# Layer 1's keys, values and masks of a two-layer attention kernel, made ahead of the layer instead of inside its steps

## The chip, the cores and the metric

The kernel runs on one core of one Trainium2 chip. The metric is the device time of one execution in microseconds (us). The core has a tensor engine (PE, with its weight loads listed as PEld), a vector engine (DVE), a scalar engine (ACT), GpSimd (POOL) and a sync engine (SP), which here issues nearly all DMAs. Each engine runs its own instruction list in order and waits on semaphores. Matmuls write PSUM, which has eight banks of 512 float columns a partition; everything else lives in SBUF.

## The reference, cut to what matters

Batches B = 32, sequence S = 128, width D = 128. Four stages change the residual x:

```
x = x + attn0(norm(x), ctx)            # 16 heads of 8, rotary, no mask
x = x + ffn0(norm(x))                  # 128 -> 512 -> 128, ternary weights
x = x + attn1(norm(x), ctx, mask)      # 16 query heads of 8, 4 key/value heads of 8
x = x + experts(norm(x))               # 8 experts, one chosen per token

attn1:  q = query @ Wq.T + bq ;  k = ctx @ Wk.T + bk ;  v = ctx @ Wv.T + bv   # k, v are 32 wide
        sim = where(causal & (adj != 0), q k^T / sqrt(8), -max) ;  softmax ; @ v ; layer norm ; @ Wo.T + bo
```

Keys, values and masks of attn1 depend on `ctx` and `adj` alone, which are inputs. They don't depend on x.

## The kernel before, in words

**The steps.** Each attention layer is a list of steps `step(t, j)`, one for a batch, with j = t mod 6. `attention(L)` (L529 on PE, L980 on ACT, L1257 on POOL, L1460 on DVE, L369 on SP) builds the step of one engine. In step t the engines work on different batches: PE makes the scores of batch t+2 (`scores`, L633), the transposed scores of t (`scoresT`, L658), the product with the values of t-1 (`pv`, L689), and the output product of t-2 (`out_project`, L745). Even steps also project the values (`project_v`, L597) and keys (`project_k`, L578) of a pair of batches, odd steps transpose the normalised x of a pair (`xn_transposes`, L538) and project its queries (`project_q`, L548). In layer 1 the odd step also makes the gate's base logits (`base_logits`, L566).

**The halves.** The scores of a batch have two halves of eight heads. Both use the one tile `score`, so `scores` of the next half waits until DVE has taken the row maxima of the last one (`maxima`, L1532, tile `negmax`). PE's order in a step is: scores half 0, scoresT half 0, pv, transposes of maxima (L729) and output (L736), then values or `xn` transposes, scores half 1, scoresT half 1, output product, regrouping (L713), then projections (L790 to L814). "First half" below is the time from scores half 0 to scores half 1 of a batch, "second half" the time from there to the next batch's half 0.

**Query and key pieces.** Queries and keys are float32, and each is cut into three bf16 pieces: ACT makes the whole (`whole`, L989, in layer 1) and the high piece (`high`, L1000), POOL the middle, the rest and the low piece (`cut`, L1272: lines L1281, L1282, L1284). SP then stacks them with six DMAs a pair of batches into `stack` (`stack_first`, `stack_last`, L404 and L415), each of which carries a query piece and a key piece. A blank row and the maxima's row (`max_rows`, L437) come in DMAs of their own. Both layers do this for every pair.

**Layer 1's masks.** For each pair SP loads `adj` (L385), DVE makes a bf16 mask (`make_mask`, L1514, line L1528; the triangle is read from PSUM, L728, from the fourth pair on), and SP copies its two halves of partitions crosswise into `swapped` (L427). PE adds both to the scores with matmuls (L619, L629). Layer 1's values come from a product of 32 columns for each batch (L608) and are put beside their bias into `Vc` by DVE (`values`, L1502).

**Between the layers.** `ffn(early)` runs 16 pairs (L817 on PE, L1143 on ACT, L1377 on POOL, L1761 on DVE). PE's pair: transposes (L825), up (L835), down (L845). From pair 8 on, each pair also runs one step of layer 1, from t = -8 on (`run_early`, L286). PE and ACT run pairs 2 to 7 in a loop (`pair_loop`, L319), and PE runs steps 6 to 23 of both layers in a loop of three rounds (`body_loop`, L291). After layer 0, SP issues four loads of expert weights (L475), a 896 KB write of zero rows (L478), and then waits for layer 1.

**In layer 1** POOL also has the bias of x (`add_bias`, L1308), reciprocal roots, and one or more indirect DMAs a step that scatter rows to the experts (`scatter`, L1334). DVE also ranks tokens, in units of two to six batches.

## Time and profile before

| | us |
|---|---|
| median of three runs (535.7 to 539.16) | 536.88 |
| the profiled execution | 535.18 |
| its span | 533.0 |
| PE busy in the span | 459.7 (86%) |
| DVE busy | 380.5 (71%) |
| POOL busy | 359.5 (67%) |
| ACT busy | 350.0 (66%) |

The span runs from the first to the last instruction of the profiled execution, and some 2 us lie around it. From the starts of the row maxima (line L1536), layer 0's attention takes the span up to about 165 us, the ffn up to 249 us (layer 1's first scores are at 240 us), layer 1's attention up to about 412 us. The experts' products begin at about 446 us. A row of the timeline gives start, duration, engine, line and operation; "x8" means that eight instructions were merged into one row. A figure in brackets is the idle time before it and what ended it.

### The profile page before, as it was taken

The numbers are of one execution on the slowest core, as the hardware profiler recorded it, in microseconds if no ns is written. First come the engines' busy times: TensorE is split into PE (matmuls) and PEld (weight loads), VectorE is DVE, ScalarE is ACT, GpSimd is POOL, SyncE is SP. The second block draws the span as 40 slices with busy tenths as digits, with TensorE's granted clock in tenths as the row PEclk, the third lists the DMA queues.
The fourth block names the chain that finished last, engine by engine and source line by source line (L and its number), as shares of the span: only waits on it lengthen the run. The fifth ranks groups of instructions, "written<-read, shape, count | busy, mean of one in ns | idle before, by whom it ended". The sixth has DMA issues, their size and how long they took to land.

```text
span 533.0 us, 19424 instructions
## 1 busy us (share of the span) xinstructions
PE 459.7 (86%) x6192; PEld 357.6 (67%) x6192; DVE 380.5 (71%) x1125; ACT 350.0 (66%) x872; POOL 359.5 (67%) x739
## 2 busy tenths in 40 slices
PE   3678999999988799998999999999978615999992
PEld 2456777777766699885566666666655405999991
DVE  6788888888986566535578888898898562555551
ACT  4366788888865556563677788788767713666661
POOL 5788887888842366577667776999986770555552
PEclk9799999999999999999799999999999955999997
DMA  7565445454432930034344444555442233444430
GB/s 182 146 160 147 109 121 124 115 138 114 124 77 59 337 85 0 1 91 104 94 114 119 127 122 113 149 146 146 126 126 70 74 121 86 106 108 108 106 99 23
DMA packets 103996, 60.18 MB, mean 113 GB/s; under 512 B 21234, under 2 KB 100098, under 8 KB 103922
## 3 DMA queue, kind: packets, MB, share of 16 engines
q1 hardware_dynamic: 100562, 51.92, 38.8%
q0 software_dynamic: 2784, 6.82, 3.7%
q8 instruction: 36, 0.59, 0.5%
q10 hardware_dynamic: 576, 0.53, 0.3%
q14 instruction: 38, 0.31, 0.2%
HBM read 20.03 MB, written 8.81 MB: 54 GB/s over the span
## 4 chain that ended last, share of the span: by engine, by line
PE 63%; POOL 11%; issue 8%; DVE 8%; DMA 5%; ACT 2%; SPq 1%; POOLq 0%; DVEq 0%; ACTq 0%
PE bank L702 8%; PE bank L923 6%; PE bank L845 5%; PE score L653 5%; PE scoreT L835 5%; PE scoreT L913 5%; PE bank L561 3%; POOL expert_rows L1341 3%; DVE negmax L1536 3%; PE bank L592 3%; PE bank L756 3%; DMA stack<-negpT 2%; PE scoreT L680 2%; PE score L913 2%; PE score L619 2%
## 5 line engine op out<-in xcount | busy, mean ns | idle before, releaser
L1536 DVE TENSOR_REDUCE negmax<-score 128x8 f32<-128x1024 f32 x128 | 156.2, 1220 | 36.1 <-PE score L653 34.1
L1028 ACT ACTIVATE P<-scoreT 128x1024 f32<-128x1024 f32 x128 | 131.7, 1029 | 51.4 <-PE scoreT L671 30.1
L702 PE MATMUL bank<-P,Vc 128*32 128x128 f32 x2048 | 69.2, 276 | 1.9 <-issue 1.8
L1420 POOL DMA_INDIRECT out<-by x39 | 37.5, 962 | 48.8 <-DVE by L1882 48.1
L702 PEld LDWEIGHTS bank<-P,Vc 128*32 128x32 f32 x2048 | 52.1, 109 | 15.4 <-issue 9.8
L653 PE MATMUL score<-stack 64*128 64x128 bf16 x1024 | 51.9, 222 | 6.9 <-DVE negmax L1536 4.5
L653 PEld LDWEIGHTS score<-stack 64*128 64x128 bf16 x1024 | 29.6, 95 | 37.8 <-issue 23.4
L1284 POOL TENSOR_TENSOR pieces<-rest,pieces 128x256 bf16<-128x256 f32 x63 | 42.8, 679 | 4.9
L1281 POOL TENSOR_TENSOR pieces<-full,pieces 128x256 bf16<-128x256 f32 x63 | 42.3, 672 | 4.7 <-ACT pieces L1008 4.4
L1282 POOL TENSOR_TENSOR rest<-full,pieces 128x256 f32<-128x256 f32 x63 | 42.5, 675 | 0.0
L923 PE MATMUL bank<-M,P 128*128 x312 | 41.5, 276 | 0.5 <-DVE by L1882 0.5
L1292 POOL TENSOR_TENSOR negp<-negmax,blank 128x16 bf16<-128x16 f32 x64 | 14.4, 225 | 38.7 <-DVE negmax L1536 36.6
L1184 ACT ACTIVATE P<-scoreT,We 128x128 f32<-128x128 f32 x104 | 29.7, 369 | 15.6 <-PE scoreT L913 15.6
L923 PEld LDWEIGHTS bank<-M,P 128*128 128x128 f32 x312 | 38.3, 193 | 0.7 <-issue 0.7
L1882 DVE SCALAR_TENSOR_TENSOR by<-bank,XB 128x128 f32<-128x128 f32 x39 | 13.7, 351 | 33.3 <-PE bank L923 33.2
L1341 POOL DMA_INDIRECT expert_rows<-XR,sloti x32 | 32.1, 1004 | 7.8 <-issue 7.0
L1044 ACT COPY negpT<-bank 128x128 bf16<-128x128 bf16 x64 | 17.0, 266 | 26.9 <-PE bank L736 20.9
L1066 ACT ACTIVATE xn<-XR,xsh,xrs 128x128 f32<-128x128 f32 (+1 forms) x64 | 29.9, 494 | 5.5 <-POOL xsh L1244 5.4
L619 PE MATMUL score<-mask,negI 64*64 64x512 bf16 x128 | 26.7, 402 | 7.3 <-DVE negmax L1536 6.3
L845 PEld LDWEIGHTS bank<-F,hT 128*128 128x128 f32 x256 | 30.9, 192 | 0.8
L1008 ACT CAST pieces<-full 128x256 bf16<-128x256 f32 x64 | 25.8, 403 | 8.2 <-POOL full L1270 7.8
L845 PE MATMUL bank<-F,hT 128*128 128x128 f32 x256 | 31.0, 275 | 0.0
(215 smaller groups left out, 1220.0 us busy)
## 6 DMA issues: line engine op xcount, KB each, us to landing
stack<-pieces SPq DMA_DIRECT2D x192, 128.0 KB, 2.5
ctxT<-in_ctxT SPq DMA_DIRECT2D x32, 128.0 KB, 2.4
XB<-expert_rows SPq DMA_DIRECT2D x39, 66.0 KB, 2.1
XA<-expert_rows SPq DMA_DIRECT2D x39, 64.0 KB
XR<-in_x SPq DMA_DIRECT2D x4, 512.0 KB, 4.8
stack<-blank SPq DMA_DIRECT2D x32, 64.0 KB, 2.1
stack<-negpT SPq DMA_DIRECT2D x64, 32.0 KB, 1.9
ME<-in_M SPq DMA_DIRECT2D x1, 2048.0 KB, 9.9
```

The lines of the kernel that those rows point to most:

```text
L619: nc.tensor.matmul(SCORE[halves(c), r, :].rearrange("p (h n) -> p h n", h=HQ), negI[halves(r), halves(r)], rows_.unsqueeze(1).broadcast_to ...
L653: mm = nc.tensor.matmul(SCORE[:, r, i * 128:(i + 1) * 128], Qs[pb][rows, h, tb * S:(tb + 1) * S], Ks[pb][rows, kv, tb * S:(tb + 1) * S], s ...
L702: mm = nc.tensor.matmul(PVOUT[VCOL * i:VCOL * (i + 1), half * 128:(half + 1) * 128], Vc[:, k % BODY, at:at + VCOL], P32[:, 2 * p_slot(L, k ...
L845: mm = nc.tensor.matmul(f_result(p, h), hT[:, b, c, h * S:(h + 1) * S], F2[:, c, :], start=(c == 0), stop=(c == FC - 1))
L923: mm = nc.tensor.matmul(bank[4 + r][:, 0:D], bhT[r][:, c * 128:(c + 1) * 128], M2[:, bass.ds(e, 1), c:c + 1, :].rearrange("p o c n -> p (o ...
L1028: nc.scalar.activation(P32[:, at:at + 2, :], SCORET[:], ACT.Exp, scale=SCALE).then_inc(sem("exp_done"), 1)
L1281: nc.gpsimd.tensor_tensor(pc[:, 1, :], f, h, ALU.subtract).then_inc(sem(f"{nm}_pieces"), 1)
L1282: nc.gpsimd.tensor_tensor(r, f, h, ALU.subtract).then_inc(sem(f"{nm}_pieces"), 1)
L1284: nc.gpsimd.tensor_tensor(pc[:, 2, :], r, pc[:, 1, :], ALU.subtract).then_inc(sem(f"{nm}_pieces"), 1)
L1341: nc.gpsimd.indirect_dma_start(out=rows_d, out_offset=bass.IndirectOffsetOnAxis(ap=sloti[:, t:t + 1], axis=0), in_=XR[:, t, :], in_offset= ...
L1420: nc.gpsimd.indirect_dma_start(out=out, out_offset=bass.IndirectOffsetOnAxis(ap=at_, axis=0), in_=by[r][:, 0:D], in_offset=None).then_inc( ...
L1536: nc.vector.tensor_reduce(negmax[:, k % 2, :, half * HQ:(half + 1) * HQ], SCORE[:].rearrange("p r (h k) -> p r h k", h=HQ), AX.X, ALU.max, ...
```

## The change

Layer 0's product for the values gets 64 more columns: layer 1's keys (32) and values (32) of the same batch. It is issued once a batch, in every step, where a pair's two products stood in the even step. ACT copies the 128 columns to `Vc` and the 64 others to a new tile `KVT`. Between the layers, PE turns the keys of all batches with eight transposes (`turn_keys`, ffn pair 1), ACT makes whole and high piece (pairs 2 to 4), DVE and POOL the other pieces (pairs 3 to 5), and SP stacks them with 24 DMAs into the key parts of the three stacks and a fourth tile. All `adj` are loaded in layer 0 into the memory of the experts' down weights `M2`, which are loaded in layer 1 instead in 16 parts. DVE makes all masks in pairs 3 to 10, into columns of XR, and SP swaps them with 12 DMAs into unused columns of `Vc`. In layer 1, POOL adds the values' bias from `KVT` (`own_values`). Projection and cutting of keys, the loads of ctx and adj, mask making and swapping are gone from its steps. Query projection and base logits move from the odd to the next even step. PE's layer 1 steps and the ffn pairs on PE and ACT are written out instead of looped.

```diff
@@ SP, layer steps
+                        row = known(p * 2)
+                        sp.dma_start(adj[:, bass.ds(row, 2), :], maskd[:, bass.ds(row, 2), :]).then_inc(sem("adj_loaded"), 16)
...
+                    else:
+                        sp.dma_start(rows_of(Qs[b], s), pieces[b][:, QSLOT[s], :]).then_inc(sem(f"stacked{L}{b}"), 16)
...
-                        load_ctx(j + 7)
-                        if L:
-                            load_adj(j + 7)
-                    if L and j % 2 == 0:
-                        swap_mask(j + 4)
+                        if L == 0:
+                            load_ctx(j + 7)
+                            load_adj(j - 1)
+                        else:
+                            load_down(j + 7)
@@ SP, after layer 0
+            sp.wait_ge(sem("k1_high"), 2)
+            sp.wait_ge(sem("k1_pieces"), 4)
+            sp.wait_ge(sem("k1_low"), 2)
+            sp.wait_ge(sem("rot_filled"), 1)
+            sp.wait_ge(sem("scoresT_ready"), 2 * B)
+            for i, tile in enumerate(K1S):
+                for s in range(SLOTS):
+                    sp.dma_start(rows_of(tile, s), k1pieces[32 * i:32 * i + 32, KSLOT[s], :]).then_inc(sem("k1_stacked"), 16)
+            sp.wait_ge(sem("pv_done"), 2 * B)
+            for s in range(BODY):
+                lo, end = BODY * s, min(BODY * s + BODY, B)
+                sp.wait_ge(sem("mask_made"), end // 2)
+                for to, at in ((0, TILE), (TILE, 0)):
+                    sp.dma_start(SWAPPED[to:to + TILE, s, 0:end - lo, :], MASK[at:at + TILE, lo:end, :]).then_inc(sem("mask_swapped"), 16)
@@ PE
+                        pe.wait_ge(sem("v_ready"), count(t))
+                        pe.wait_ge(sem("kv_ready"), count(t))
+                        if h == 0 and is_pair(p + 1):
+                            pe.wait_ge(sem("xnT_ready"), p + 2)
+                        nc.tensor.matmul(VAL, ctxT[b][:, h * S:(h + 1) * S], WV[:], start=True, stop=True
+                                         ).then_inc(sem("v_projected"), 1)
...
+                        if L and t == 0:
+                            pe.wait_ge(sem("k1_stacked"), K_STACKED)
+                            pe.wait_ge(sem("mask_made"), PAIRS)
+                            pe.wait_ge(sem("mask_swapped"), SWAPPED_ALL)
...
-                    if j % 2 == 0:
-                        project_v(j + 4, t)
-                    else:
-                        xn_transposes(j + 7)
+                    if j % 2 == 1:
+                        xn_transposes(j + 7, t)
+                    if L == 0:
+                        project_v(t + 4, j + 4)
                     scores(t + 2, 1, j + 2)
                     scoresT(t, 1, j)
                     out_project(t - 2, j - 2)
                     regroup(t - 1)
-                    if j % 2 == 0:
+                    if L == 0 and j % 2 == 0:
                         project_k(j + 6, 0)
                         project_k(j + 6, 1)
-                    else:
-                        if L:
-                            base_logits(j + 7)
+                    elif L == 0:
                         project_q(j + 7, 0)
                         project_q(j + 7, 1)
+                    elif j % 2 == 0:
+                        base_logits(j + 6)
+                        project_q(j + 6, 0)
...
+                def turn_keys():
+                    pe.wait_ge(sem("kv_ready"), B)
+                    for g in range(GROUPS1):
+                        mm = nc.tensor.transpose(bank[5 + g // 4][:, g % 4 * 128:(g % 4 + 1) * 128],
+                                                 KVT[:, 0, 4 * g:4 * g + 4, :].rearrange("p t n -> p (t n)"), eye[:])
@@ ACT
+                        act.wait_ge(sem("v_projected"), t + 1)
+                        nc.scalar.copy(row, VAL[:, D:D + KV].rearrange("p (x n) -> p x n", x=2)).then_inc(sem("kv_ready"), 1)
...
+                    if p in (2, 3):
+                        whole_keys(p - 2)
+                    if p in (3, 4):
+                        high_keys(p - 3)
@@ POOL
+                        nc.gpsimd.tensor_tensor(v, KVT[:, 1, 2 * p:2 * p + 2, :].rearrange("p b (h d) -> p b h d", d=DK), bias, ALU.add
+                                                ).then_inc(sem("v1_ready"), 1)
...
+                if p in (4, 5):
+                    low_keys(p - 4)
@@ DVE, ffn pairs
+                    if p in (3, 4):
+                        cut_keys(p - 3)
+                    if 3 <= p < 11:
+                        make_masks(4 * (p - 3), 4 * (p - 3) + 4)
...
+                    for dst in (k1pieces[:, 1, at], k1rest):
+                        nc.vector.tensor_tensor(dst, k1full[:, n, :], k1pieces[:, 0, at], ALU.subtract).then_inc(sem("k1_pieces"), 1)
...
+                    dve.wait_ge(sem("adj_loaded"), 16 * PAIRS)
+                    for t in range(lo, end, 2):
+                        nc.vector.scalar_tensor_tensor(MASK[:, t:t + 2, :], adj[:, t:t + 2, :], 0.0,
+                                                       upper[:].unsqueeze(1).broadcast_to([128, 2, 128]), ALU.is_equal, ALU.max
+                                                       ).then_inc(sem("mask_made"), 1)
```

## Rows read from the trace of the kernel before

**Rows 1.** Stretches: us, busy (x) of PE, PEld, DVE, ACT, POOL, PE clock, DMA share, GB/s
```profile
62.00:139.00 77.00, 76.57 (x1380) 59.12 (x1374) 67.30 (x127) 65.24 (x143) 62.38 (x143) 1.00 0.49 123
178.00:241.00 63.00, 59.90 (x413) 54.56 (x413) 33.74 (x166) 36.16 (x95) 38.82 (x81) 1.00 0.31 81
253.50:404.00 150.50, 143.36 (x2243) 93.21 (x2238) 126.02 (x325) 114.81 (x262) 118.53 (x256) 0.98 0.49 126
```

**Rows 2.** The chain that ended last, in order of time: start, us, what
```profile
187.48 1.73 PE scoreT L835 x8
189.21 1.78 PE bank L845 x16
```

**Rows 3.** Timeline of layer 0, ACT's exponentials
```profile
105.35 1.02 ACT L1028 ACTIVATE P<-scoreT 128x1024 f32<-128x1024 f32 x1 [0.26 <-PE scoreT L680]
```

**Rows 4.** Timeline of PE in layer 1: three batches, first scores rows of each half
```profile
359.10 0.40 PE L619 MATMUL score<-mask,negI 64*64 64x512 bf16 x1
...
361.40 0.53 PE L608 MATMUL bank<-W1V,ctxT 128*128 128x32 f32 x4
361.86 0.40 PE L619 MATMUL score<-mask,negI 64*64 64x512 bf16 x1
...
363.52 0.60 PE L592 MATMUL bank<-ctxT,W1K 128*128 128x256 f32 x2
364.05 0.40 PE L619 MATMUL score<-mask,negI 64*64 64x512 bf16 x1
...
366.66 0.40 PE L619 MATMUL score<-mask,negI 64*64 64x512 bf16 x1
...
368.32 0.51 PE L575 MATMUL bank<-Wc,xnT 128*128 128x8 f32 x4
...
369.29 0.40 PE L619 MATMUL score<-mask,negI 64*64 64x512 bf16 x1
...
372.41 0.23 PE L729 MATMUL bank<-eyeb,negp 128*128 128x128 bf16 x1 [0.93 <-POOL negp L1297]
```

**Rows 5.** Timeline of DVE in the same stretch of layer 1
```profile
362.64 1.23 DVE L1536 TENSOR_REDUCE negmax<-score 128x8 f32<-128x1024 f32 x1 [0.60 <-PE score L653]
...
365.00 0.23 DVE L1512 TENSOR_TENSOR Vc<-bank,rowsb 128x64 f32<-128x64 f32 x1
365.14 1.21 DVE L1536 TENSOR_REDUCE negmax<-score 128x8 f32<-128x1024 f32 x1
```

**Rows 6.** Groups by line and shape: busy us, mean ns, idle before and its releasers
```profile
L1281 POOL TENSOR_TENSOR pieces<-full,pieces 128x256 bf16<-128x256 f32 x63 | 42.3, 672 | 4.7 <-ACT pieces L1008 4.4
...
L1528 DVE SCALAR_TENSOR_TENSOR mask<-adj,bank 128x256 bf16<-128x256 int32 x13 | 5.5, 421 | 0.3
...
L1528 DVE SCALAR_TENSOR_TENSOR mask<-adj,upper 128x256 bf16<-128x256 int32 x3 | 1.3, 435 | 0.0
...
L1498 DVE TENSOR_TENSOR rest<-full,pieces 128x256 f32<-128x256 f32 x1 | 0.9, 892 | 0.0
```

**Rows 7.** Timeline of the ffn: DVE's normalised x, and PE's transposes
```profile
203.99 0.57 DVE L1457 TENSOR_SCALAR fxn<-XR,fmv,frstd 128x128 f32<-128x128 f32 x2
...
205.75 0.38 PE L825 MATMUL score<-eye,fxn 128*128 128x128 f32 x2
```

**Rows 8.** Timeline of SP after layer 0
```profile
171.12 12.74 SPq L478 DMA_DIRECT2D expert_rows<-blank  x1
...
229.66 1.25 SPq L413 DMA_DIRECT2D stack<-pieces  x2
230.95 1.26 SPq L434 DMA_DIRECT2D swapped<-mask  x2
```

**Rows 9.** Timeline of PE in layer 1's early steps
```profile
235.90 0.61 PE L575 MATMUL bank<-Wc,xnT 128*128 128x8 f32 x4 [0.46 <-ACT xnT L987]
...
240.49 0.40 PE L619 MATMUL score<-mask,negI 64*64 64x512 bf16 x1
```

More of the change, by code:

```diff
@@ L133, in build @@
         M2 = sb("M2", [128, EXPERTS, FC, 128])
+        adj = M2[:].bitcast(I32).rearrange("p e c n -> p (e c) n")
         rank = sb("rank", [128, EXPERTS])
         ctxT = [sb(f"ctxT{i}", [128, PAIR]) for i in range(3)]
-        adj = [sb(f"adj{i}", [128, 2, 128], I32) for i in range(3)]
-        mask = sb("mask", [128, BODY, 128], BF16)
-        swapped = sb("swapped", [128, BODY, 128], BF16)
         xst = sb("xst", [128, B, 6])
@@ L148, in build @@
         xsd = sb("xsd", [128, B])
-        rotA = [sb(f"rotA{i}", [128, PAIR]) for i in range(2)]
-        rotB = [sb(f"rotB{i}", [128, PAIR]) for i in range(2)]
+        rot = sb("rot", [128, 4, PAIR])
+        rotA, rotB = [rot[:, i, :] for i in range(2)], [rot[:, 2 + i, :] for i in range(2)]
         full = [sb(f"full{i}", [128, PAIR]) for i in range(2)]
@@ L156, in build @@
         Ks = [s[:, :, 1, :] for s in stack]
+        KVT = sb("KVT", [128, 2, B, KV // 2])
+        K1S = [s[:, :, 1, :] for s in stack] + [rot[:].rearrange("p c n -> p (c n)").bitcast(BF16).rearrange("p (h n) -> p h n", h=8)]
         Vc = sb("Vc", [128, BODY, HEADS * VCOL])
+        SWAPPED = Vc[:].bitcast(BF16)[:, :, 2 * KV1 * VCOL:].rearrange("p s (b n) -> p s b n", n=S)
         negmax = sb("negmax", [128, 2, 2, HEADS // 2])
@@ L266, in both_pieces, with swapped, key_of @@
             return pieces[b][:, q:k + 1:k - q, :]
+        def swapped(t):
+            return SWAPPED[:, t // BODY, t % BODY, :]
+        def key_of(t, half):
+            g = t // 4
+            return K1S[t % 4][:, half * GROUPS1 // 2 + g // 2, g % 2 * S:(g % 2 + 1) * S]
         def f_turned(p, b):
@@ L379, in load_ctx @@
                     if is_pair(p):
-                        read, column = known(p + P0 - 2), known(p * PAIR)
+                        read, column = known(2 * p - 4), known(p * PAIR)
                         sp.wait_ge(sem("v_projected"), count(read))
@@ L423, in stack_last @@
                                 sp.wait_ge(sem("q_pieces"), low)
-                                sp.wait_ge(sem("k_pieces"), low)
-                            sp.dma_start(rows_of(stack[b], s), both_pieces(b, s)).then_inc(sem(f"stacked{L}{b}"), 16)
-                def swap_mask(k):
-                    p, b = pair(k), turn(k)
-                    if is_pair(p):
-                        slots = slice(k % BODY, k % BODY + 2)
-                        sp.wait_ge(sem("mask_made"), known(p + 1))
-                        for lo, hi in ((0, TILE), (TILE, 0)):
-                            sp.dma_start(swapped[lo:lo + TILE, slots, :], mask[hi:hi + TILE, slots, :]
-                                         ).then_inc(sem(f"mask_swapped{b}"), 16)
+                                if L == 0:
+                                    sp.wait_ge(sem("k_pieces"), low)
+                            stack_slot(b, s)
                 def max_rows(t, k):
@@ L627, in masks_of_scoresT @@
                             at = r ^ c
-                            rows_ = (mask, swapped)[c][halves(r), k % BODY, :]
+                            rows_ = (MASK[:, t, :], swapped(t))[c][halves(r), :]
                             nc.tensor.matmul(SCORET[:, r, :].rearrange("p (h q) -> p h q", h=HQ)[:, :, halves(at)], rows_,
@@ L724, in max_transpose @@
                         pe.wait_ge(sem("negmaxT_ready"), count(t + T0))
-                        if L and k % 2 == 1 and is_pair(pair(k + 3)):
-                            pe.wait_ge(sem("mask_made"), count(pair(k + 3) + 1))
-                        if L and isinstance(t, int) and t == 1:
-                            nc.tensor.matmul(UPPER, eyeb[:], upper[:], start=True, stop=True)
                         nc.tensor.transpose(MAXT, negp[:].rearrange("p r d h -> p (r d h)"),
@@ L1026, in exps @@
                         act.wait_ge(sem("pv_done"), count(2 * (t + T0) + half - 2))
+                        if L and t == 0 and half == 0:
+                            act.wait_ge(sem("k1_stacked"), K_STACKED)
                         at = 2 * p_slot(L, k, half)
@@ L1346, in step @@
                     split_max(t + 1, j + 1)
[L1347 removed]
                     if L and j % 2 == 1:
                         out_rstd((t - 3) // 2)
[L1350 removed]
+                    elif L:
+                        cut(j + 4, 0)
+                    elif j % 2 == 0:
+                        cut(j + 4, 1)
+                    else:
+                        cut(j + 5, 0)
                     if L == 0:
```

283 lines of the change are left out of this document (141 added, 142 removed).

## The prediction

> **What bounds the kernel now.** I read the stretches first, then the timeline of PE and DVE inside one pair of batches of each layer, then the groups by line, then SP's queue. In layer 0's steady stretch PE is busy 76.57 of 77 us, and in the ffn 59.90 of 63 [rows 1]. In both, PE's own work is the length of a step. In layer 1, from batch 34's first maximum to batch 62's, PE is busy 143.36 of 150.5 us, DVE 126, POOL 118.5, ACT 115 [rows 1]: PE leads, but not by much. That is 14 pairs of batches, so 10.75 us a pair.
>
> Which wait ends last there is read from the halves. The scores' first mask matmuls start at 359.10, 361.86, 364.05, 366.66 and 369.29 [rows 4]: the even batch's first half lasts 2.76 us and its second 2.19, the odd batch's 2.61 and 2.63, in sum 10.19. A maximum starts 0.78 us after its scores' start (361.86 to 362.64), takes 1.23, and the next scores start 0.18 after its end (363.87 to 364.05) [rows 4, 5]. This loop through the single score tile allows no half under 2.19, so the even second half is already at the loop's length, and the three others are longer because of PE's own work. The missing 0.56 us a pair (10.75 less 10.19) are waits in some pairs: the clearest is PE standing 0.93 us for POOL's split of the maxima [rows 4], behind POOL's key and query cuts, square roots and scatters.
>
> **What the change removes in layer 1.** PE loses, per pair, the values' two products (361.40 to 361.86, 0.46 us) from the even first half and the keys' product (363.52 to 364.05, 0.53) from the even second half. Base logits and queries (368.32 to 369.29, 0.97) move from the odd second half into the even second half [rows 4]. DVE loses 0.42 for the mask and 0.22 for the values, POOL one cut of three instructions of 0.67 [rows 5, 6] and gains a small bias sum of 128x64, no row of which is on POOL: between 0.2 and 0.67, I take 0.3, because it has a quarter of a cut's elements. ACT loses two copies a pair. SP loses five issues a pair and gains one.
>
> The new halves:
> - Odd second half: PE has 2.63 - 0.97 = 1.66 left, so the loop and DVE set it. From one maximum's start to the next one's, with the output's normalisation between, DVE takes 2.50 with the values' instruction (362.64 to 365.14). That instruction adds the 0.14 from 365.00 to 365.14 [rows 5]. Without it, and without the mask, 2.36.
> - Even first half: PE has 2.76 - 0.46 = 2.30. The loop gives 1.22 + 0.18 + 0.78 = 2.18 between the maxima, that is 2.35 between the scores' starts. So 2.18.
> - Even second half: 2.19 - 0.53 + 0.97 = 2.63, PE's.
> - Odd first half: unchanged, 2.61, PE's.
>
> Sum 9.78 a pair, 0.41 under today's 10.19. PE sheds 0.99 us a pair, but more than half of it comes off halves in which the loop through the score tile is next to last. The other part is the 0.56 us of waits. POOL's relief of 1.7 us a pair should end most of those. Against that, the token ranking's instructions on DVE now stand in halves without PE work to hide them. Between the ends, 0 and 0.56, I take 0.32. A pair is then 10.1, and 14 x (10.75 - 10.1) = 9.1 us less. Ends: at 9.78, 13.6 us less; with the waits kept whole (10.34), 5.7 less.
>
> **What it adds in layer 0.** A product of 256 columns costs 1.73/4 = 0.43 us of PE, one of 128 columns 1.78/8 = 0.22 [rows 2], so 64 more columns cost 0.106, and 32 products 3.4 us. PE is the bound in the steady part [rows 1]. At both ends of the layer there are waits that can take some of it. I take 3.0, with ends 1.5 and 3.4. ACT gets a second copy a batch and copies values batch by batch, some 0.3 us a step. Its exponential stands idle 0.26 us for PE in one half [rows 3] and the step itself grows, so I take 0, and up to 0.1 a step (3 us) as the upper end. The 16 loads of adj add 128 KB a pair to DMAs that are busy 49% of the time [rows 1]: 0.
>
> **Between the layers.** PE's eight transposes: two show 0.38 us busy [rows 7], so up to 1.5. They are pipelined, I take 1.0. Pairs 8 to 15 lose two values' products (0.46) and three keys' products (0.53), 2.5 us, and the stand of 0.46 us before the base logits [rows 9] goes three times, since they now come a step after the xn transposes: 1.4. Some of it lies beside the first maxima; I count 3.2 less.
>
> DVE is the new risk. Its normalised x is done at 204.56 and PE's transposes that need it start at 205.75 [rows 7], a slack of 1.19 us a pair. Two masks, 0.84, fit in. In pairs 3 and 4 come two subtractions of 128x512 each. No row has this shape; from 256 columns, 0.42 [rows 6] gives 0.84 each, and the slowest row of 256 columns with two SBUF inputs, 0.89, gives 1.78. At the lower value, which is nearer to the other DVE rows, DVE is 0.84 + 1.68 - 1.19 = 1.3 us late in each pair, 2.7 in all; at the upper 3.2 a pair, 6.4. If this work were hidden it would be 0. I take 2.7. ACT's four passes over 512 columns have idle time in the pairs (36 of 63 us busy), as has POOL (39 of 63) [rows 1]. The memory fill of `rot` stands in POOL's idle time before the pairs.
>
> Sum of the stretch: 1.0 - 3.2 + 2.7 = 0.5 more.
>
> SP: 24 key stacks and 12 swaps stand in front of layer 1's first issue. They can start when POOL's second low piece is made, pair 5, near 207 us. At 0.62 us an issue (1.25 for two) they end at 229, which is when layer 1's first stacking starts today, 229.66 [rows 8]. I take 0. Loops written out on PE: 0.4 us less, from steps at the loop's edge in which PE starts a little late.
>
> **The sum.** On the profiled execution's time: 535.2 + 3.0 + 0.5 - 9.1 - 0.4 = 529.2. The profiled execution is 1.7 under the median of the runs, so the predicted median is 531.0 (1.1% less). About 1%, 5.4 us, is what a measurement of this kernel can tell from no change.
>
> **A rule against the change.** The masks and cuts run on DVE with two SBUF inputs, while today 13 of 16 masks read the triangle from PSUM: 0.435 us against 0.421 [rows 6], hardly a difference, but the one 256-column subtraction with two SBUF inputs took 0.892 us. If DVE had to wait there for a POOL instruction, 0.67 us at most for a cut's size [rows 6], then the masks' 0.84 + 0.67 would overrun the slack of 1.19 by 0.32 in each of eight pairs, 2.6 us. The time would be 533.6. The Trainium skill ("SBUF — State Buffer", Who interferes with whom) states this lock: a DVE instruction with two SBUF inputs and a GpSimd instruction that reads SBUF block one another. By that rule it is 533.6, by the mask rows 531.0.
>
> **The rivals.**
> - *All waits go.* Layer 1 reaches 9.78 a pair (13.6 less), layer 0 costs only 1.5, the cuts are hidden: 535.2 + 1.5 - 2.2 - 13.6 - 0.4 = 520.5, median 522 to 525. For it: every engine is relieved in layer 1, and the stack's DMAs halve. Against it: the ranking work on DVE, 126 of 150.5 busy.
> - *The relief lands on the loop.* Halves that lose PE work are held by DVE, the ranking instructions lengthen them, and a pair stays at 10.5: 3.5 less, while layer 0 costs 3.4 and ACT adds 1: 535.2 + 3.4 + 1 + 0.5 - 3.5 = 536.6, median 538. For it: PE work moves from an odd half into an even one, which becomes 2.63 where it was 2.19.
> - *DVE and POOL block one another*: 533.6, as above.
> - *Slower: SP is late.* The one queue takes 36 DMAs before it may stack layer 1's first queries. If they queue up like the 896 KB write that held SP for 12.74 us [rows 8], 14 us a MB, the 2.6 MB take 37 us from 207, to 244. Seven issues and a landing follow, some 7 us, and the first scores, at 240.49 today [rows 9], come at 251 or later, where without this they would come near 238: 13 us. The median would be 544. It decides from the moment that the last swap is issued after about 233 us. Against it: such transfers read and write SBUF only, few bytes each, and the DMAs are nearly idle then.
>
> **Chances.** Forecast 0.42, all waits go 0.23, relief on the loop 0.20, DVE against POOL 0.08, SP late 0.07. The forecast's own range is 527.5 to 535; somewhat over half of it is under 531.5. So faster by over 1%: 0.50; within 1%: 0.43; slower by over 1%: 0.07. The range for 8 in 10 is 524 to 538.5. It leaves out the lower half of the first rival and the last.
>
> **What would show it.** Right: maxima in layer 1 that start 2.63 and 2.61 us after the last in an even second and an odd first half, and 2.2 to 2.4 in the two others; PE no longer idle for POOL's split; layer 0's steps 0.1 us longer each; a gap of PE over 1 us before the transposes of ffn pairs 5 and 6. Wrong: scores of layer 1's first batch waiting for the stacked keys or the swapped masks; ACT without idle time before its exponentials in layer 0; a pair in layer 1 still over 10.5 us.

## The result, and the profile after

The changed kernel takes 534.61 us (median of 20 runs, 530.98 to 539.82), the kernel before 538.71 in the 20 runs beside them (534.19 to 543.95). The ratio is 0.9922, with a 95% interval of 0.9899 to 0.9946: 0.8% faster. The profiled executions stand closer together than the medians: 534.26 (span 532.5) after and 535.18 before, which lay 3.5 under its own median. So the gain is read from the medians, and the profiles tell where it comes from.

The stretches of the kernel after, with the columns of [rows 1]: the same 77 us of layer 0, and layer 1 from batch 36 on.

```profile
66.00:143.00 77.00, 75.19 (x1335) 57.17 (x1337) 64.61 (x124) 66.00 (x165) 59.90 (x141) 1.00 0.52 134
273.00:403.00 130.00, 123.34 (x2038) 78.09 (x2032) 109.45 (x288) 101.38 (x227) 91.83 (x215) 1.00 0.31 80
```

Layer 1, where the gain is. The timeline of DVE after, in batches 38 to 40, answers to [rows 5]:

```profile
280.74 1.23 DVE L1599 TENSOR_REDUCE negmax<-score 128x8 f32<-128x1024 f32 x1 [0.72 <-PE score L687]
...
283.10 1.23 DVE L1599 TENSOR_REDUCE negmax<-score 128x8 f32<-128x1024 f32 x1
...
285.25 1.23 DVE L1599 TENSOR_REDUCE negmax<-score 128x8 f32<-128x1024 f32 x1 [0.34 <-PE score L687]
...
287.88 1.22 DVE L1599 TENSOR_REDUCE negmax<-score 128x8 f32<-128x1024 f32 x1 [0.19 <-PE score L687]
...
290.50 1.22 DVE L1599 TENSOR_REDUCE negmax<-score 128x8 f32<-128x1024 f32 x1 [0.72 <-PE score L687]
```

Between the maxima: 2.36, 2.15, 2.63, 2.62. The bracket tells who set each half. 283.10 has none: DVE came straight from its own chain. The others waited for PE's scores; in the half that ends at 285.25 PE had no gap either, so which of the two sets that one isn't told apart. PE's timeline shows the other side of the first one; the idle figure ahead of the even scores is PE waiting for the maximum at 280.74 to end (281.97), and the queries and base logits stand in the even second half:

```profile
281.40 0.38 PE L750 MATMUL bank<-eye,outs 128*128 128x128 f32 x2
282.06 0.37 PE L652 MATMUL score<-XR,negI 64*64 64x512 bf16 x1 [0.29 <-issue]
...
286.13 0.51 PE L616 MATMUL bank<-Wc,xnT 128*128 128x8 f32 x4
286.49 0.68 PE L601 MATMUL bank<-xnT,W1Q 128*128 128x256 f32 x2
```

The first maxima of batches 16 and 26 (layer 0), 36 and 62 (layer 1), before and then after:

```profile
96.62 1.22 DVE L1536 TENSOR_REDUCE negmax<-score 128x8 f32<-128x1024 f32 x1 [0.33 <-PE score L653]
139.17 1.22 DVE L1536 TENSOR_REDUCE negmax<-score 128x8 f32<-128x1024 f32 x1
264.83 1.22 DVE L1536 TENSOR_REDUCE negmax<-score 128x8 f32<-128x1024 f32 x1
403.89 1.22 DVE L1536 TENSOR_REDUCE negmax<-score 128x8 f32<-128x1024 f32 x1
```

```profile
99.50 1.22 DVE L1599 TENSOR_REDUCE negmax<-score 128x8 f32<-128x1024 f32 x1 [0.25 <-PE score L687]
142.85 1.22 DVE L1599 TENSOR_REDUCE negmax<-score 128x8 f32<-128x1024 f32 x1
273.34 1.22 DVE L1599 TENSOR_REDUCE negmax<-score 128x8 f32<-128x1024 f32 x1
403.70 1.22 DVE L1599 TENSOR_REDUCE negmax<-score 128x8 f32<-128x1024 f32 x1
```

Ten batches of layer 0 went from 42.55 to 43.35 us. Thirteen pairs of layer 1 went from 139.06 to 130.36, 8.7 less. That first profile is the best one: four others whose layer 1 has the same steps (all below) have 132.38, 133.90, 135.67 and 135.82 there, and a second one of the old steps has 139.51. The last three of the four and the 139.51 are from one chip, so there 3.7 to 5.6 us are gained.

Between the layers, DVE after (ffn pairs 3 to 5), then PE's transposes that wait for it, to be read beside [rows 7]:

```profile
202.56 1.26 DVE L1871 TENSOR_TENSOR P<-P 128x512 bf16<-128x512 f32 x2
203.74 0.75 DVE L1877 SCALAR_TENSOR_TENSOR XR<-M,upper 128x256 bf16<-128x256 int32 x2
...
208.30 1.29 DVE L1871 TENSOR_TENSOR P<-P 128x512 bf16<-128x512 f32 x2 [1.31 <-POOL P L1476]
...
212.65 1.75 DVE L1877 SCALAR_TENSOR_TENSOR XR<-M,upper 128x256 bf16<-128x256 int32 x2
```

```profile
205.85 0.44 PE L851 MATMUL score<-eye,fxn 128*128 128x128 f32 x2 [0.61 <-DVE fxn L1550]
...
211.67 0.43 PE L851 MATMUL score<-eye,fxn 128*128 128x128 f32 x2 [1.86 <-DVE fxn L1550]
```

The second key cut waits 1.31 us for POOL's low piece of the first half, because both halves go through the one tile `k1rest`. SP after, beside [rows 8]: stacking starts at 214.27 and not near 207 (at 210.87 in the second profile), the last swap is issued at 238.8, and the first issue for layer 1 comes at 239.50.

```profile
214.27 11.95 SPq L511 DMA_DIRECT2D stack<-P  x18
...
230.14 9.32 SPq L517 DMA_DIRECT2D Vc<-XR  x12
239.50 1.11 SPq L412 DMA_DIRECT2D M<-in_M  x2
```

### The profile page after: what moved, and what is told of

It reads as the page before. It is cut to its first block, busy times and chain, and to the rows that moved or that the text cites. A ratio compares the mean times of both kernels' runs of the same rounds, so it can differ in the third digit from the quotient of the medians.

```text
span 532.5 us, 18987 instructions
## 1 busy us (share of the span) xinstructions
PE 451.1 (85%) x6103; PEld 347.1 (65%) x6103; DVE 378.0 (71%) x1113; ACT 348.0 (65%) x892; POOL 336.7 (63%) x710
## 4 chain that ended last, share of the span: by engine, by line
PE 61%; DVE 10%; DMA 8%; issue 8%; POOL 6%; SPq 4%; ACT 1%; DVEq 0%; POOLq 0%; ACTq 0%
PE bank L739 9%; PE bank L963 6%; PE score L687 5%; DMA stack<-pieces 5%; PE scoreT L953 5%; PE scoreT L861 4%; PE bank L871 4%; DVE negmax L1599 4%; DMA stack<-negpT 3%; PE bank L601 3%; PE score L652 3%; PE bank L788 3%; PE score L953 2%; PE scoreT L714 2%; PE scoreT L662 2%
## 5 line engine op out<-in xcount | busy, mean ns | idle before, releaser
L687 PE MATMUL score<-stack 64*128 64x128 bf16 x896 | 44.9, 220 | 9.6 <-DMA stack<-pieces 5.0
L687 PEld LDWEIGHTS score<-stack 64*128 64x128 bf16 x896 | 25.7, 95 | 38.7 <-issue 22.7
L1343 POOL TENSOR_TENSOR pieces<-full,pieces 128x256 bf16<-128x256 f32 x47 | 31.6, 672 | 7.4 <-ACT pieces L1050 6.5
L652 PE MATMUL score<-XR,negI 64*64 64x512 bf16 x128 | 26.9, 405 | 10.8 <-DVE negmax L1599 6.0
L1346 POOL TENSOR_TENSOR pieces<-rest,pieces 128x256 bf16<-128x256 f32 x47 | 31.9, 679 | 3.7
L1344 POOL TENSOR_TENSOR rest<-full,pieces 128x256 f32<-128x256 f32 x47 | 31.7, 674 | 0.0
L861 PE MATMUL scoreT<-fxnT,F 128*128 128x256 f32 x120 | 30.2, 397 | 0.4 <-ACT hT L1203 0.3
```

The lines of the kernel that those rows point to most:

```text
L652: nc.tensor.matmul(SCORE[halves(c), r, :].rearrange("p (h n) -> p h n", h=HQ), negI[halves(r), halves(r)], rows_.unsqueeze(1).broadcast_to ...
L687: mm = nc.tensor.matmul(SCORE[:, r, i * 128:(i + 1) * 128], Qs[pb][rows, h, tb * S:(tb + 1) * S], keys[rows, :], start=(L == 0), stop=True ...
L861: mm = nc.tensor.matmul(f_hidden(p, c), F1[:, c * 128:(c + 1) * 128], fxnT[:, b, :], start=True, stop=True)
L1346: nc.gpsimd.tensor_tensor(pc[:, 2, :], r, pc[:, 1, :], ALU.subtract).then_inc(sem(f"{nm}_pieces"), 1)
```

## The experiments

The experiments ran in four sets, each on a chip of its own. Every set was run beside the kernel before, whose median was 546.03, 539.23, 541.42 and 542.23 us in the four sets. So ratios are compared between sets, and microseconds only inside one. Line numbers are those of each kernel.

**Layer 0's added columns, made 128 instead of 64.**

```
-        WV = sb("WV", [128, D + KV])
+        WV = sb("WV", [128, PAIR])
-            (eyeb[:], a["eyeb"]), (WV[:], a["WV"]),
+            (eyeb[:], a["eyeb"]), (WV[:, 0:D + KV], a["WV"]), (WV[:, D + KV:], a["WV"][:, 0:PAIR - D - KV]),
```

> The changed kernel, with layer 0's values product 256 columns wide instead of 192; the 64 more repeat the first 64 of the weights and nobody reads them. My theory: layer 0 is bound by PE, 64 columns cost 0.106 us of PE in each of 32 products, so the stretch from batch 0's first maximum to batch 31's grows from 143.95 us by 2.6 to 3.4, and the whole time by as much (535.2 to 538, where the changed kernel has 534.6). Rival: the products' columns are hidden, and the 5.5 us that layer 0 gained through the change come from its DMAs or from ACT; then the stretch and the time stay within 1 us of the changed kernel's.

Measured: 1.0018 of before (0.9982 to 1.0054), 546.13 us. Its maxima of batches 16 and 26:

```profile
101.81 1.23 DVE L1599 TENSOR_REDUCE negmax<-score 128x8 f32<-128x1024 f32 x1 [0.25 <-PE score L687]
146.23 1.22 DVE L1599 TENSOR_REDUCE negmax<-score 128x8 f32<-128x1024 f32 x1
```

44.42 us for ten batches where the changed kernel has 43.35: 0.107 a batch for 64 columns. That is the predicted 0.106, and layer 0 is PE's. From batch 0 to 31 it took 147.49 us, 3.5 more than the changed kernel's 143.95. The rival falls. The whole time rose by more than the text has, by 0.0096 in the ratio or 5.2 us, and with these intervals anything from 2 to 8 us; only the steady part shows the price of the columns.

**The loads of adj taken out of layer 0.**

```
-                            load_adj(j - 1)
...
+            for c in range(4):
+                sp.dma_start(adj[:, 8 * c:8 * c + 8, :], maskd[:, 8 * c:8 * c + 8, :]).then_inc(sem("adj_loaded"), 16)
```

> The changed kernel, with the 16 loads of adj taken out of layer 0 and issued as 4 loads right behind it, ahead of the experts' loads. My theory (as predicted: these loads cost layer 0 nothing): from batch 0's first maximum to batch 31's stays 143.95 us within 1 us, its irregular stalls (near batches 1, 3, 5, 11, 12, 13) stay, and the masks on DVE may wait for 2 MB of loads behind layer 0, up to 3 us more in all. Rival: the loads of adj hold back layer 0's stacking DMAs, and the irregular 2.9 us of the stretch go: about 141 us, and the time falls by 1 to 3 us unless the masks wait.

Measured: 0.9973 (0.9932 to 1.0014). Batches 16 to 26 take 43.35 us as with the loads, batches 0 to 31 143.44. Ten profiles of kernels whose layer 0 has these loads and 192 columns run from 142.26 to 146.41. So in the steady part they cost nothing, and the irregular stalls didn't go with them; an effect under a microsecond on the whole layer can't be told from this. The whole ratio is no better than the changed kernel's 0.9922, so no gain from moving the loads is shown.

**The masks away from the key cuts.**

```
-                    if 3 <= p < 11:
-                        make_masks(4 * (p - 3), 4 * (p - 3) + 4)
+                    if 5 <= p < 13:
+                        make_masks(4 * (p - 5), 4 * (p - 5) + 4)
...
+                if p in (4, 5):
+                    low_keys(p - 4)
                 ffn_rstd(p + 4, b)
                 ffn_bias(p + 2)
-                if p in (4, 5):
-                    low_keys(p - 4)
```

> The changed kernel, with the masks made in ffn pairs 5 to 12 instead of 3 to 10, so that they don't stand behind the key cuts in pairs 3 and 4, and with POOL's low key pieces ahead of its square roots of the same pair instead of behind them. My theory: DVE is late in pairs 3 to 6 by 3.2 us in sum; without the masks there most of it goes, and the stretch from batch 31's second maximum to batch 32's first shrinks from 79.8 us by 2 to 3, the time with it. Rival: PE's transposes there wait for something that the masks don't set (the lower TensorE clock, or ACT), or later pairs lose as much to the masks: the stretch stays within 0.7 us.

Measured: 1.0141 (1.0077 to 1.0205), slower than before and 8 us over the wide kernel of the same set. PE's waits from 166 us to layer 1 (waited for: us in sum, times, longest), this kernel, and then the changed one:

```profile
PE score L652 <- DMA stack<-pieces: 5.2, 1, 5.2
PE score L851 <- DVE fxn L1550: 2.1, 2, 1.1
```

```profile
PE score L851 <- DVE fxn L1550: 3.5, 3, 1.9
```

The stalls fell by 1.4 us as meant, but the stretch that was to shrink by 2 to 3 us took 82.09 where the changed kernel has 79.80. The reason is that layer 1's first scores now waited 5.2 us for the stack, and SP's timeline says why:

```profile
207.78 11.93 SPq L511 DMA_DIRECT2D stack<-P  x18
...
223.62 17.71 SPq L517 DMA_DIRECT2D Vc<-XR  x12
241.38 1.11 SPq L412 DMA_DIRECT2D M<-in_M  x2
```

Key stacking started at 207.78, near the prediction's 207, once POOL's low pieces came first. The 12 swaps took 17.71 us instead of 9.32, because they waited 9.2 us for masks now made two pairs later, and everything behind them in SP's one queue came later. In the changed kernel the first stack's pieces are issued until 245.07, and the first scores start at 247.23 without a wait:

```profile
241.31 3.76 SPq L442 DMA_DIRECT2D stack<-pieces  x6
...
247.23 0.40 PE L652 MATMUL score<-XR,negI 64*64 64x512 bf16 x1
```

In the spread kernel PE was ready at 243.4 (its first scores came at 248.55, less the wait of 5.16), the pieces were issued until 246.95, and the scores followed 1.6 us later. By that measure the changed kernel's pieces were there at 246.7: the cover left over the swaps is about 0.5 us, an estimate. Why the whole kernel lost more than these 5.2 us isn't settled. One part stands at the start of layer 1: from batch 32 to 36 it took 28.27 us at a mean granted clock of 0.68, where the wide kernel of the same set took 25.09 at 0.80.

**The same, with the swaps out of the way.** PE now waits for each group of swaps by itself.

```
+            swap(0)
+            body_loop(sp, attention(1), before={2 * s - 6: partial(swap, s) for s in range(1, BODY)})
```

> The kernel with the masks in pairs 5 to 12 and the low key pieces first, which ran before and was slower, and now SP swaps only the first of six groups of masks ahead of layer 1 and the five others between its steps. My theory: that kernel lost 5.2 us because SP stood 9.2 us for the last masks ahead of layer 1's first stacking. With this the wait of batch 0's scores for the stack goes, layer 1's first issue comes before 232 us, and the time is 1 to 3 us under the changed kernel (DVE's stalls of 3.5 us down to 2.1). Rival: the issue in the early steps is held by something else (POOL's query pieces, the stack being read), and the wait stays over 3 us: slower than the changed kernel by 3 us or more.

Measured: 0.9880 (0.9847 to 0.9914), 533.46 us beside 534.41 for the changed kernel in the same set. The wait for the stack is gone from the list of waits, and layer 1's first issue came at 227.98. SP then stood until 240.07 for POOL's query pieces, which is what the rival names, only earlier than it hurts: the scores came at 246.28. So the loss of the last kernel was SP's queue, as said. That this one also beats the changed kernel isn't shown: the intervals overlap.

**The loops alone.** The kernel before, with PE's layer 1 and both loops over the ffn pairs written out.

```
-            body_loop(pe, early, EARLY - AHEAD, {B + 4: counts}, LAST)
+            body_steps(early, EARLY - AHEAD, LAST, {B + 4: counts})
-                    pair_loop(pe, step)
+                    every_pair(step)
-                return {B - 2: first_evac, B: first_relus}, partial(pair_loop, act, step)
+                return {B - 2: first_evac, B: first_relus}, partial(every_pair, step)
```

> The kernel before, with PE's layer 1 loop, and PE's and ACT's loops over the ffn pairs, written out as the change does, and nothing else. My theory: 0.4 us less than before, within what can be measured: 0 to 1. Rival: the written-out steps carry more of the gain, or cost by more instruction fetches: over 2 us to either side.

Measured: 1.0030 (0.9991 to 1.0068); batches 36 to 62 took 139.51 us, where before has 139.06. None of the gain is here. The predicted 0.4 us is 0.07%, which is too little to be told from nothing.

**The changed kernel again.**

> The changed kernel once more, as the measure for the others of this set and for a second profile. My theory: a ratio to before near the first one (0.992), layer 0 from batch 0's to batch 31's first maximum 142.5 to 144 us, and the halves of layer 1 at 2.15, 2.63, 2.61 and 2.36 again; what differs between profiles of layer 1 is waits for the stack. Rival: the gain of the first measurement was that chip's: a ratio of 0.998 to 1.002 here.

Measured: 0.9930 (0.9900 to 0.9961). The gain repeats. Most halves of layer 1 are again 2.15, 2.63, 2.61 and 2.36; what differs is mainly single halves of 3.2 to 4.2 us. In this stretch the transposed scores wait 3.5 us in sum for a DMA.

**Layer 1's transposes moved behind the scores.**

```
-                    if j % 2 == 1:
+                    if j % 2 == 1 and L == 0:
                         xn_transposes(j + 7, t)
...
                     scores(t + 2, 1, j + 2)
+                    if j % 2 == 1 and L:
+                        xn_transposes(j + 7, t)
```

> The changed kernel, in which layer 1's two transposes of the normalised x come one place later in PE's odd step: behind the scores of the second half (and ahead of its transposed scores) instead of ahead of them. My theory of the halves: the odd first half (2.61 us) is set by PE, the odd second (2.36) by DVE with PE idle 0.29, so moving 0.43 us of PE work from the one to the other makes them 2.18 and 2.36 to 2.5: 0.3 to 0.4 a pair, 13 to 16 pairs, 4 to 6 us less than the changed kernel run beside it. Rival: what sets the time of layer 1 is the chain over POOL, ACT and SP that brings the maxima into the stack and the key and query pieces behind it; then the gain comes back as waits of scoresT for the stack, and the sum is within 1.5 us of the changed kernel.

Measured: 0.9948 (0.9917 to 0.9978), 537.10 us beside 534.41. Neither text: the odd first half fell to 2.39, and the odd second rose to 2.78, the whole 0.42 of the moved work. DVE's timeline shows it:

```profile
291.41 1.23 DVE L1601 TENSOR_REDUCE negmax<-score 128x8 f32<-128x1024 f32 x1 [0.50 <-PE score L687]
292.96 0.26 DVE L1610 RECIPROCAL rden<-bank 128x16 f32<-128x16 f32 x1 [0.32 <-PE bank L750]
...
294.19 1.22 DVE L1601 TENSOR_REDUCE negmax<-score 128x8 f32<-128x1024 f32 x1
```

The odd second half is DVE's chain from the regrouped output (reciprocal, normalised output, statistics) to the next maximum. It starts with PE's regrouping (L750), and this had been done 0.2 us before the maximum ended. PE idle in a half doesn't mean that work put anywhere in that half is free: ahead of the regrouping it lengthens DVE's chain, behind it it fills the 0.29.

**The transposes behind the regrouping**, in the steps without a ranking, and ACT's copy behind its second exponential.

```
                     regroup(t - 1)
+                    if j % 2 == 1 and late(L, t):
+                        xn_transposes(j + 7, t)
...
                     exps(t, 1, j)
+                    if j % 2 == 1 and late(L, t):
+                        evac_xnT(j + 7, t)
```

> The changed kernel, in which layer 1's two transposes of the normalised x come at the end of PE's odd step, behind the regrouping of the output, and ACT's copy of them behind its second exponential; the odd steps with a token ranking, and the early ones, stay as they are. What the moved transposes of the first try showed: behind the scores they delayed the regrouping, DVE's reciprocal waited 0.3 us for it, and the odd second half went from 2.36 to 2.78. My theory now: DVE's chain from the regrouped output to the next maximum (1.13 us between two maxima) sets that half, and PE has 0.29 us idle only behind the regrouping; so here the odd first half is 2.39 or less and the odd second stays 2.36 to 2.5: 0.1 to 0.25 a pair, 1 to 2.5 us under the changed kernel (ratio 0.988 to 0.991 where that has 0.993). Rival: ACT's later copy and normalisation push its next exponential, and PE waits there: odd halves of 5.1 us and more in sum, ratio 0.994 or above.

Measured: 0.9854 (0.9809 to 0.9899). Where nothing else waits (batches 38 to 41) the halves are 2.15, 2.63, 2.39 and 2.36, in sum 9.53 instead of 9.75, as this theory has them. The whole stretch from batch 36 to 62 doesn't show it: it took 131.16 us, between the changed kernel's 130.36 and 132.38. The ratio lies under the changed kernel's, but the intervals touch. So the gain is shown in the halves and not in the whole.

**Transposes behind the scores, base logits half a step earlier.**

```
-                    elif j % 2 == 0:
-                        base_logits(j + 6)
-                        project_q(j + 6, 0)
+                    elif j % 2 == 0:
+                        project_q(j + 6, 0)
+                    else:
+                        base_logits(j + 7)
```

> As the run with the moved transposes, and besides the base logits' two products moved from the even batch's second half to the odd batch's second half, half a step earlier for the same pair, DVE waiting for them before it reads the output of an odd batch. My theory: even second half 2.63 to 2.18, odd second 2.36 to 2.5 or 2.6, so 0.2 to 0.3 a pair less than with the moved transposes alone, 3 to 4 us, and 7 to 10 us less than the changed kernel. Rival: the chain of the maxima's stacking decides: no gain over the moved transposes, within 1.5 us.

Measured: 0.9864 (0.9831 to 0.9897), 532.71 us. The even second half fell from 2.63 to 2.36 and the odd second stayed at 2.78: the base logits stand behind the regrouping, and there they cost nothing. This shows that the 2.63 was PE's work. The gain over the changed kernel is 1.7 us in its set, not 7 to 10. PE stands 0.29 us in a pair whose halves are 2.15, 2.63, 2.61 and 2.36. So by an estimate an order of the same work can give no more than that a pair, 4 us in all, and beyond it only what waits are left.

**The moves together.**

> The kernel with the transposes and base logits moved (0.986 of before) and the one with spread masks and swaps between the steps (0.988) in one; the swaps of groups 3 to 6 share one wait at batch 12. My theory: the two gains lie in different stretches, layer 1's steady pairs (129.9 us from batch 36 to 62) and the end of the ffn (76.4 us), so they add: 0.980 to 0.984 of before. Rival: both shorten the same low-clock stretch at the start of layer 1, or the swaps collide with the stacking: 0.986 to 0.990.

> The kernel with the late transposes, with the spread masks, the low key pieces first and the swaps between the steps. My theory: adds its gain of 0.005 to that of the late transposes alone: 0.983 to 0.987 of before. Rival: 0.988 or above, if the late transposes bring nothing.

Measured: 0.9846 (0.9806 to 0.9886) and 0.9891 (0.9829 to 0.9953), 532.61 and 537.06 us. That the gains add isn't shown: the first lies just above the 0.980 to 0.984 of the text, and the second within its rival. The first is the fastest of the study by its ratio, with six runs, and its interval lies under that of the changed kernel in either of its two sets (0.9899 to 0.9946, 0.9900 to 0.9961).

**The maxima's row first in SP's step.** Built on the first of these two. The chain of waits of the changed kernel in one of its long halves had shown this order of events (start, us, what):

```profile
302.84 0.69 POOL pieces L1343
...
303.54 0.53 SPq L442
...
304.12 0.61 SPq L442
...
304.78 0.03 SPq L460
...
304.84 3.44 DMA stack<-negpT
```

```
                 def step(t, j):
+                    if L:
+                        max_rows(t + 1, j + 1)
                     if j % 2 == 0:
                         blank_max(j + 4)
```

> The kernel with transposes, base logits, masks and swaps all moved (0.985 of before), and in layer 1 SP issues the maxima's row of a batch first in each of its steps, ahead of the stack's blank row and pieces instead of behind them. In the profiles of layer 1 the longest halves (3.0 to 4.2 us where 2.3 to 2.6 is the rule) are waits of the transposed scores for the DMA of the maxima's row; its issue stood behind two issues of query pieces (0.53 and 0.60 us), and these behind POOL's cut. My theory: the maxima's row is ready long before, so these waits (2.6 us in that kernel, 1.4 to 4.9 in the others) fall under 0.5, batch 36 to 62 goes from 129.7 to 126 to 127.5 us, and the ratio to 0.978 to 0.983. Rival: the maxima's row is itself late (POOL's split, PE's transpose, ACT's copy), and the pieces, now behind it, come late instead: waits for the stack's pieces of the same size, and no gain or a loss (0.984 or above).

Measured: 1.0957 (1.0914 to 1.1001), 50 us slower than before. The waits of PE and of SP over 130 us of layer 1:

```profile
PE score L660 <- DMA stack<-pieces: 25.0, 9, 3.7
```

```profile
SPq L461 <- ACT negpT L1103: 63.4, 18, 5.5
```

The rival holds, and far beyond its size. In the kernel that it was built on SP waited 11.7 us for ACT's `negpT`, here 63.4. The maxima's row of the next batch is made late in a step; with its wait ahead, SP can't send the pieces that are ready, and they come after the scores want them (chain: `negpT` at 323.66, then four issues of 0.53 to 0.60 and a DMA of 2.04, scores at 328.64). That PE then stands still costs a second time: the granted clock over 130 us is 0.86 where it was 1.00.

## Why the prediction was right, and where it was off

531.0 was predicted, 534.61 measured; the difference to before was predicted as 5.9 us on the median first shown and is 4.1. The forecast case is the one that happened, at the far end of its own range (527.5 to 535), and the gain of 0.8% fell into the class "within 1%", which had 0.43 against 0.50 for "faster by over 1%".

By stretches the two profiles of the changed kernel differ from the one of before as follows (us):

| | predicted | first | second |
|---|---|---|---|
| batch 0 to 31 | +3.0 | +5.5 | +3.8 |
| batch 31 to 36 | -0.1 | +4.0 | +2.0 |
| batch 36 to 62 | -8.9 | -8.7 | -6.7 |
| all else | 0 | -1.3 | -2.2 |
| span | -6.0 | -0.5 | -3.1 |

The first of the 14 predicted pairs (0.65) stands in the second row, the 13 others and the 0.4 for the loops in the third. The second profile is from another chip than the two others. So the terms of the second row were too small by 2 to 4 us and layer 0's by 1 to 2.5. That the total stayed near is in part luck: the rest of the kernel, for which the sum had nothing, came out shorter.

- **Layer 1's halves.** Predicted 2.18, 2.63, 2.61 and 2.36; measured 2.15, 2.63, 2.61 and 2.36. Who sets each one is right too, by the brackets and by the two moved-work kernels (2.63 to 2.36 without the base logits, 2.61 to 2.39 without the transposes, DVE's chain in the odd second). Predicted 0.65 less a pair; measured 0.67 in the first profile (8.7 in 13 pairs) and 0.51 in the second (6.7). The other three profiles with these steps have 0.25 to 0.40, so the term was too large, by about a third in the mean of the five (0.42). Its two parts were both off. The halves gave more than said: the usual pair of before has 2.76, 2.50, 2.29 and 2.80 between its maxima, 10.35 in sum where the one pair of [rows 4] gave 10.19, and the usual pair after has 9.75, so 0.60 less and not 0.41. The waits gave nothing: over the usual pair a pair of before lost 0.35 and 0.38 us (two profiles), one of after 0.28 to 0.70 (five). "PE no longer idle for POOL's split": that wait is gone (2.0 us before). In its place come waits for the maxima's DMA, 1.4 and 3.5 us in the two profiles and 3.2 to 4.9 in the others, against 0.3 and 1.0 with the old steps. The prediction didn't have them.
- **Layer 0.** The price of 64 columns is right: 0.106 predicted, 0.107 from the wide kernel. Over ten steady batches the change cost 0.080 a batch. The term of 3.0 was small all the same: from batch 0 to 31, the ten profiles mentioned have 144.4 in the mean, the two of the kernel before and its written-out form 138.5 and 141.2. That is 4.6 more, with 2.7 between two profiles of one layer 0, so 1.6 over the term and inside its scatter. ACT and adj at nothing: right in the steady part.
- **DVE beside the key cuts.** Predicted 2.7 us of stalls in two pairs; measured 0.61 + 1.86 = 2.5. The sum is right by luck, and of the two gaps of over 1 us that the text names only one came. There were two errors. A cut took 0.684 us and not 0.84, and the second pair's stall holds a wait of 1.31 for POOL that no step had: POOL's low piece stood behind its square roots and a bias, and DVE behind that.
- **PE's eight transposes, 1.0.** The ffn pair that holds them is 0.88 us longer than before in the second profile (from one pair's transposes to the next, 4.78 against 3.90). In the first it is 2.5 us longer (6.39): there TensorE's clock had fallen, as the last section shows.
- **Early steps, 3.2 less.** Right. From PE's transposes of pair 10 to layer 1's first scores it is 31.00 us before (209.49 to 240.49) and 27.70 after (219.53 to 247.23), 3.3 less, and 27.71 in the second profile. What the sum lacked comes behind it. At the start of layer 1 PE has nothing beside the maxima and stands 1.33 and 1.52 us for them, and its clock goes down behind that. The stretch from batch 32 to 36 took 23.56 us before and 25.33 after (24.93 in the second profile), a term of +1.8 and +1.4.
- **SP.** "From 207 to 229, cost 0": the cost is right, the times aren't. Stacking started at 214.27 since POOL's low piece was late, and the last swap was issued at 238.8, 10 us later than said. It cost nothing because the ffn just covers it; in the spread kernel, where it didn't, PE stood for 5.2 us. The rival "SP is late" had 0.07 and named 233 us as the point from which it decides; the swaps went past this at no cost. Its mechanism is real (PE stood for the stack, though not because of the transfers' size), its point was set too early.
- **DVE and POOL block one another** (533.6, 0.08). Its number is near the result, its mechanism as priced isn't what happened: no transposes waited in pairs with masks alone. But one mask did pay: of 16 masks the shortest took 0.390 us, the median 0.416, and the longest 1.380. It is the second of the two that start at 212.65 and ran from 213.02 to 214.40, while POOL's low piece ran from 212.78 to 214.12:

```profile
L1877 DVE SCALAR_TENSOR_TENSOR XR<-M,upper x16: 390/416/1380, 203.7 to 233.6; 128x256 bf16<-128x256 int32 x16
...
203.36 1.34 POOL L1301 TENSOR_TENSOR xrs<-xsd,powers 128x4 f32<-128x4 f32 x1
...
212.78 1.34 POOL L1476 TENSOR_TENSOR P<-P 128x512 bf16<-128x512 f32 x1
```

  The mask reads two SBUF tiles, started 0.24 us behind POOL's instruction and ended 0.28 behind it. The Trainium skill ("SBUF — State Buffer", Who interferes with whom) says that DVE and GpSimd share a port pair under an exclusive lock; this pair of rows agrees with it, and no run took the overlap away to prove it. It isn't so for every instruction of POOL: the two masks at 203.74 took their usual 0.75 together, beside the one of POOL on four columns that ran from 203.36 to 204.70. The long mask cost PE nothing here: the next transposes (215.74) had no wait.
- **Written-out loops, 0.4 less.** Measured 1.0030 with 0.9991 to 1.0068 around it. A gain of over 0.1% is ruled out; 0.4 us is less than that and stays open.

What stays open: layer 0's irregular stalls between batches 1 and 13, which differ from profile to profile, and why the maxima's DMA comes late in layer 1.

## What to carry to other kernels

Split a pipelined step at its repeated landmark (here the row maxima) and ask of each piece which engine's chain fills it; removed work pays only in the pieces that this engine sets. Idle time has a place in the order: the same 0.43 us of PE work cost 0.42 in front of the instruction that starts DVE's chain and nothing behind it. In a queue that waits in order, a transfer is moved with everything behind it: look at when its own input is ready before putting it first, and at what stands behind it before making its input later.

## What the hardware showed that was not expected

- **TensorE's clock at the start of layer 1.** In the changed kernel PE was busy 0.74 us of the 3 us ahead of the fall. Behind it the granted clock is 0.56 in the mean of 3 us and then 0.50 up to 268 us, which is 1.2 in place of 2.4 GHz:

```profile
256.00:259.00 3.00, 0.74 (x12) 0.37 (x12) 2.15 (x3) 1.30 (x4) 1.74 (x5) 1.00 0.29 77
259.00:262.00 3.00, 2.25 (x19) 0.97 (x19) 1.35 (x2) 0.51 (x1) 2.48 (x7) 0.56 0.00 0
```

  The whole stretches from batch 32's to batch 36's first maximum, of the changed kernel, of the kernel before with its loops written out, and of the fastest of the study:

```profile
248.01:273.34 25.33, 20.03 (x211) 12.73 (x211) 13.19 (x26) 8.74 (x19) 11.22 (x33) 0.80 0.20 52
```

```profile
244.47:266.15 21.68, 17.85 (x223) 12.24 (x224) 14.17 (x31) 10.12 (x23) 14.96 (x40) 1.00 0.39 98
```

```profile
250.77:271.71 20.94, 16.19 (x211) 10.95 (x211) 13.28 (x27) 8.45 (x18) 11.55 (x35) 1.00 0.30 73
```

  These two kept the full clock; the 12 others of the 14 profiles had 0.68 to 0.86 in the mean there, and took 23.6 to 28.3 us. The kernels differ, so this alone doesn't say that the fall comes by chance here: the five profiles with the changed kernel's own start of layer 1 all had 0.79 or 0.80 and took 24.9 to 25.3 us. But between the layers one and the same program did go both ways. The first profile of the changed kernel has there, behind gaps of PE of 0.38 and 0.98 us:

```profile
186.00:189.00 3.00, 1.94 (x7) 1.43 (x8) 2.74 (x15) 2.10 (x6) 1.61 (x3) 0.78 0.33 21
189.00:192.00 3.00, 3.00 (x14) 2.52 (x13) 0.75 (x5) 1.41 (x4) 1.60 (x3) 0.65 0.00 0
```

  The second profile has the same two gaps and kept 1.00 from 182 to 194 us, and its pair with the eight transposes took 4.78 us instead of 6.39. So a pair of single profiles can differ there by 1.6 us for no reason in the kernels.
- **A DMA that lands late.** The DMA of the maxima's row in layer 1 of the changed kernel:

```profile
DMA to landing us min/median/max: 1.9/1.9/3.4
```

  The one of 3.4 is the one on the chain shown, issued right behind two DMAs of pieces into the stacks. What delayed it wasn't tried.
